# A wait split in two: high products wait for high copies, low products for low copies

## The reference: one decoder layer

```
x = x + attention(layernorm(x))        # 16 heads of 64, causal
x = x + cross_attention(layernorm(x))  # 64 context rows, one head of 256, masked
x = x + ffn(layernorm(x))              # silu gate 256->1024, two gelu layers 1024->1024, 1024->256
```

## Time and profile before

| what | us |
|---|---|
| median of the runs | 1432.95 |
| the profiled execution, its own time | 1431.65 |
| its span (first to last instruction) | 1429.6 |
| TensorE matmul busy | 1414.0 (99%) |
| VectorE busy | 1205.9 (84%) |
| ScalarE busy | 1010.3 (71%) |
| GpSimd busy | 605.3 (42%) |

### The profile page before, as it was taken

How to read it: one execution, slowest core, us unless ns; L and a number is a source line. 1 busy time by engine, 2 the same in 40 slices (tenths; PEclk the granted TensorE clock), 3 DMA queues, 4 the chain that set the end, 5 groups by cost and what they waited for, 6 DMA issues and landing times.

```text
span 1429.6 us, 29169 instructions
## 1 busy us (share of the span) xinstructions
PE 1414.0 (99%) x10408; PEld 1202.3 (84%) x10408; DVE 1205.9 (84%) x3004; ACT 1010.3 (71%) x2382; POOL 605.3 (42%) x883
## 2 busy tenths in 40 slices
PE   8999999999999999999998999999999999999998
PEld 7888888888888888888887788888888888888887
DVE  8998999989989899898899777788866757888886
ACT  7888888888888888888887854565455545555644
POOL 4676777767667767777645121111212100000000
PEclk9999999999999999999999999999999999999999
DMA  5000101001001010010022544553333583141310
GB/s 163 2 1 2 61 1 47 15 2 60 2 16 45 2 61 2 1 61 2 16 75 79 192 157 153 199 176 133 129 129 120 203 299 119 36 144 63 116 58 33
DMA packets 78277, 113.54 MB, mean 79 GB/s; under 512 B 4768, under 2 KB 54304, under 8 KB 77216
## 3 DMA queue, kind: packets, MB, share of 16 engines
q1 hardware_dynamic: 78112, 111.32, 22.7%
HBM read 71.45 MB, written 42.99 MB: 80 GB/s over the span
## 4 chain that ended last, share of the span: by engine, by line
PE 77%; ACT 13%; DVE 6%; issue 2%; POOL 2%; DVEq 0%; ACTq 0%; POOLq 0%
PE bank L1614 14%; PE bank L1446 8%; PE bank L1448 7%; PE bank L877 6%; PE bank L929 6%; ACT P L1012 5%; PE bank L879 5%; PE bank L878 5%; PE bank L1632 4%; PE bank L941 4%; PE bank L954 3%; PE bank L957 3%; ACT PT L981 3%; PE bank L1567 2%; PE bank L1558 2%
## 5 line engine op out<-in xcount | busy, mean ns | idle before, releaser
L1012 ACT ACTIVATE P<-P,stats 128x384 f32<-128x384 f32 (+3 forms) x512 | 290.2, 575 | 101.6 <-DVE stats L1114 100.3
L1144 POOL TENSOR_SCALAR P<-P,stats 128x128 f32<-128x128 f32 (+3 forms) x512 | 268.9, 542 | 113.8 <-DVE stats L1122 111.3
L1114 DVE CUSTOM_DVE_ANT_0 P<-bank,cmask 128x256 f32<-128x256 f32 (+3 forms) x512 | 216.5, 485 | 0.4
L1028 DVE TENSOR_TENSOR PT<-bank,PT 128x512 fp32r<-128x512 f32 (+1 forms) x384 | 206.8, 593 | 7.1 <-ACT PT L981 5.6
L1614 PE MATMUL bank<-op,ws 128*128 128x512 f32 x896 | 205.9, 389 | 0.0
L1446 PE MATMUL bank<-Hb,hw 128*128 128x512 f32 x512 | 201.2, 393 | 0.0
L1614 PEld LDWEIGHTS bank<-op,ws 128*128 128x128 f32 x896 | 167.3, 188 | 34.1
L981 ACT ACTIVATE PT<-bank 128x512 fp32r<-128x512 f32 (+1 forms) x384 | 172.4, 527 | 4.6 <-PE bank L941 3.9
L1448 PE MATMUL bank<-Hb,hw 128*128 128x512 f32 x448 | 174.7, 390 | 0.0
L929 PE MATMUL bank<-K,Q 64*128 64x512 f32 (+3 forms) x1536 | 140.7, 327 | 0.6 <-DVE Q L1028 0.4
L929 PEld LDWEIGHTS bank<-K,Q 64*128 64x128 f32 x1536 | 118.1, 185 | 18.9 <-issue 1.2
(11 more groups left out here) (249 smaller groups left out, 3349.0 us busy)
## 6 DMA issues: line engine op xcount, KB each, us to landing
h_scratch<-go SPq DMA_DIRECT2D x64, 256.0 KB, 2.1
src<-h_scratch SPq DMA_DIRECT2D x16, 1024.0 KB, 7.3
xs<-x_scratch SPq DMA_DIRECT2D x15, 512.0 KB, 4.1
ws<-ws_scratch SPq DMA_DIRECT2D x7, 1024.0 KB, 7.8
x_scratch<-x SPq DMA_DIRECT2D x8, 512.0 KB, 3.0
x_scratch<-xs SPq DMA_DIRECT2D x8, 512.0 KB, 3.3
xg<-x_scratch SPq DMA_DIRECT2D x8, 512.0 KB, 4.6
out<-xg SPq DMA_DIRECT2D x16, 256.0 KB, 2.1
```

The lines of the kernel that those rows point to most:

```text
L1012: e.activation(p, p, ACT.Exp, bias=st_[:, k:k + 1], scale=-1.0, accum_out=st_[:, 8 + k:9 + k]).then_inc(s_exp, 1)
L1028: return e.tensor_tensor(dst, a, b.bitcast(f32), ALU.subtract)
L1114: e.tensor_tensor_reduce(P_tile(P, i, a), banks["S", P, S_ITEM[i]][a][:, slice(*S_COLS[i])], cmask[:, 512 - n:512], -1.0, 3.0e38, ALU.add, ...
L1144: e.tensor_scalar(p, p, stats[P % 4][:, k:k + 1], 1.0, ALU.mult, ALU.mult).then_inc(s_norm, 1)
```

## The change

Only `weighted` is changed. The high product j waits for the high copies of the blocks that it reads, and the low product j for the low copies; the waits ahead of the whole sum are gone. No instruction that computes is added, removed or moved.

```diff
             w.wait_ge(s_vlo, 4 * (P // 4) + 4)
-            for u in (a, 2):
+            for j in range(4):
                 for h in range(2):
-                    w.wait_ge(s_ptlo, plo_at[P, u, h])
-            for j in range(4):
+                    w.wait_ge(s_pthi, hi_at[P, 2 if j == 2 else a, h])
                 e.matmul(out[:, 128 * j:512], V[:, j, P % 4, a * 128:a * 128 + 128],
                          PT[:, a, 0, OFF[j]:OFF[j] + 512 - 128 * j], start=j == 0, stop=j == 3)
             for j in (3, 0, 1, 2):
+                for h in range(2):
+                    w.wait_ge(s_ptlo, plo_at[P, 2 if j == 2 else a, h])
                 m = e.matmul(out[0:64, 128 * j:512], V[:, j, P % 4, a * 128:a * 128 + 64],
                              PT[:, a, 1, OFF[j]:OFF[j] + 512 - 128 * j], start=False, stop=j == 2,
                              skip_group_check=True)
```

## The result

The change makes the kernel slower: 1434.97 us in the median of 22 runs (1433.47 to 1438.8), against 1432.48 (1431.93 to 1433.88) for 22 runs of the kernel before (the three given above are among them). The ratio is 1.0018, with a 95% interval of 1.0012 to 1.0024, so about 2.5 us. The forecast was 1432.5 with a range up to 1434.2, and 0.89 for a difference within 0.2%. The difference is within 0.2%, but the median lies outside the range and on the other side than forecast. The prediction was wrong by a small amount, in the direction of too little cost. It also took 0.2% for what can be told from no change; with 22 runs of each the interval is 0.06% to either side, and leaves no doubt of the sign.

What follows compares the result with a forecast made beforehand. TensorE's matmul stream, busy 99% of the span, was taken as the bound. The median 1432.95 less 0.45 us of kept gain, plus 0 for the added waits, gave 1432.5 us, range 1431.0 to 1434.2.

Steps and rivals of the forecast that it cites:

- Step 1: Weighted sums: the wait for low copies moves to the fifth product in 60 of 64 second sums, mostly stays in first.
- Step 2: Stalls in the weighted sums of pairs 23, 36, 45, 46, 39 and 1: 0.67 us can be won.
- Step 3: Pair 36's first sum: late start and slow group, 0.59 us, stay, as its bank waits for a low copy.
- Step 4: Weighted sums: 128 products gain waits, 85 stand-alone waits are added; price taken as 0, bounds named 1.3 and 11.5 us.
- Step 5: Behind the sums, VectorE can lose earlier starts; two thirds of the 0.67 us counted as kept, 0.45 us.
- Rival A: VectorE, copying without a break at pairs 23 and 36, takes all the gain back: 1432.95 us; chance 0.26.
- Rival B: Added waits at third and fifth products cost weight loads: 11.5 us, 1444.0 us; chance 0.07 past 1436.3 us.
- Rival C: All idle time before line 954, 2.6 us including pair 36's 0.59, is won: 1430.35 us; chance 0.02.
- Rival D: A shifted stream loses or catches a stretch of lowered clock; chance 0.05, divided by sign 0.02 and 0.03.
- The signs of being wrong: In attention: quiet pairs change their step of 11.6 us, or pair 36's stall disappears.

Runs made afterwards that it cites:

- the kernel with the split alone: Changed kernel with its split waits, each product waiting with one condition instead of two, so 6 extra stand-alone waits instead of 85: 1432.04 us, ratio 0.9998.
- 85 late waits: Kernel before plus 85 satisfied stand-alone waits, only in the weighted sums of pairs 53 to 61: 1434.27 us, ratio 1.0015.
- 171 late waits: Changed kernel plus 171 satisfied stand-alone waits in the weighted sums of pairs 53 to 62: 1432.54 us, ratio 1.0000.
- the change with its fetches put back: Changed kernel, all its waits kept, with 42 fewer warm-up transposes (84 instructions) at the program's start: 1432.12 us, ratio 0.9996.
- the waits alone: Kernel before plus 85 satisfied stand-alone waits, in the weighted sums where the change has its own, without the split: 1434.11 us, ratio 1.0014.

## Why the prediction was wrong

**Step 1, where the waits go**, was right: pair 36's first sum still starts late, for the bank's claim.

**Step 2, the 0.67 us that can be won**, was right at each of its places, as the rows of after show.

**Step 3, pair 36's 0.59 us stay**, was right.

**Step 4, the price of the added waits, is the step that failed.** It said "I take 0, as pair 24 is the commoner case and the new waits ask for things that are old". For the time an instruction takes in the queue this was true: the 128 products with new conditions and the 85 stand-alone waits cost nothing inside the sums, and even 256 do not (ratio 1.0002). That a product's second condition on a semaphore makes an instruction of its own is what the two splits show, 446 stand-alone waits against 367. And what the step says of late weights behind a wait is in the trace of before at pair 36: the second product's weight load starts 0.08 us behind the first product (450.65 and 450.57), and in pair 24 0.00 (311.59 and 311.59); the starts of the two products are 0.31 and 0.23 us apart. What the step left out is that instructions have to be brought in (q8: 107 packets, 1.75 MB), and that a transfer of data which a packet meets can land later (the store of `go`, 6.6 us instead of 5.2). The sum had no term for it. It is 1.2 to 1.3 us in the profiles at one place, and 2.5 us in the medians for the change (1434.97 - 1432.48). The row that would have raised the question, q8, was on the page. A reader could not have foretold that the packet hits this store, since the point of each fetch would have had to be followed through the program; but a term with a size (one wait of a microsecond or more, somewhere behind the change) and a chance could have been had. That ought to have gone into the upper bound.

**Step 5, two thirds of the gain kept**, was too hopeful at the three places that were followed. Rival A, with a chance of 0.26, described what happens there: in the kernel with the split alone 0.15 of pair 23's 0.18 us is given back at the next transposes, and all of what pairs 45 and 46 won. The changed kernel gives back the same. For the whole of attention it isn't decided: the kernel with the split alone is at 0.9998, and 0.67 us is too small for the medians to tell how much of it is kept.

**Rival B** was named for the slower side, and it gave the right sign for a wrong reason: quiet pairs have not changed their steps (pair 24: 0.58 and 0.59), and nothing idles before the low products. Nor do the added conditions hold a weight load back there: in pair 24 that of the third product, which now carries one, starts with the product ahead of it (312.56 and 312.55). The size of the additional time is also not its 11.5 us. **Rival C** fell with pair 36. **Rival D**, the clock, did not take place either. The kernel before has a granted clock of 0.50 from 769.1 to 775.9 us (0.51 over 769 to 776), and 0.05 went to a shifted stream that loses this stretch or catches another. The changed kernel has 0.50 from 759.4 to 762.8 and from 773.1 to 776.5, about the same 6.8 us in all, and its mean granted clock is 0.997, as before.

**The signs of being wrong** that the prediction named, a changed step of the quiet pairs and the end of pair 36's stall, did not appear. Both were looked for in attention, where the change is; a loss behind it had no sign of its own.

Of the fetch itself the traces show packets of 16,384 bytes, and the kernel with 256 waits that so many instructions are one packet. TensorE hardly stands still for its instructions: between 100 and 750 us its matmul queue idles once in the kernel before for more than 0.15 us, for 0.35 us at pair 36. A transfer of data that meets the packet is not hidden in the same way. How the packet delays it is the author's estimate, from the packet's 0.9 us and the rate behind it: 23 GB/s is about a sixteenth of the rate ahead, which fits one DMA engine of the sixteen that is late with its share when the others are done. That this engine is the one which brought the instructions is argued, not shown, as the trace doesn't give the engine; nor is it shown why the delay is 1.3 to 1.5 us and the packet only 0.9.

**What stays open.** The profiles of the changed kernel and of the one with 85 late waits show steps of 1.2 and 1.3 us at the place, while their medians lie 2.5 and 2.1 us above the kernel before. The profile is a single execution. Part of the rest comes with the clock that the timed runs were granted. In the runs timed with the late waits the kernel before takes 1431.94 us in the median of its 14 runs at a mean clock of 0.997 or more and 1434.38 in the 7 at 0.996; the kernel with 85 late waits takes 1433.73 (6 runs) and 1436.14 (5 runs). The loss is 1.8 us in either group, and not 2.1. At 0.997 and more the kernel with 171 late waits takes 1432.54 (11 runs), 1.2 us less than the one with 85, which is the size of the step. But the changed kernel, sorted so when it was measured again, lies 2.2 us above the kernel before (1433.79 and 1431.63), so a part of its loss has no place yet. Nor was it tried to take the place itself away, with a third buffer beside the two halves of `go`; a shift might then still hit another transfer.

None of the versions beats the kernel before beyond its interval. The two that had a reason to, the split with one condition and the change with its fetches put back, are at 0.9998 and 0.9996.

## What to carry to other kernels

When a change adds or removes instructions of an engine whose stream is fetched while it runs, it moves the later fetches (here 85 waits in attention moved one from 819.5 to 815.6 us); a difference of 0.1 to 0.2% far from the edit can be this and nothing else, as it was here (1.0014 with the waits alone, 0.9996 with the fetches put back). Before such a difference is given to the edit, find the first place where the streams part, look for a fetch packet beside a transfer that is waited for, and put the fetches back by as many neutral instructions elsewhere (or fill up to a whole packet, 256 instructions here). And a gain of a few tenths of a microsecond ahead of an engine that feeds the next step without slack can be given back there (0.15 of 0.18 us behind pair 23): follow it to the next wait before counting it.

## What the runs showed of the hardware

- The 256 KB store of `go` for which ScalarE waits took 5.2 to 5.3 us from issue to landing in seven kernels, and 6.5 to 6.7 in the five in which a fetch packet of TensorE (16 KB, 0.9 us) started 3.0 to 3.3 us behind its issue. The store issued next took 2.9 to 3.0 us without the packet and 4.3 to 4.5 with it.
- Behind such a packet, in the changed kernel, the DMA engines' rate fell from about 400 GB/s to 23 and stayed there for 1.4 us until the store had landed; in the kernel before, without it, the rate went to nothing in about 0.5 us, for the same 1.57 MB.
- Stand-alone waits that were already satisfied took 0.106 us from one to the next. In one block of 85 they left TensorE idle for 7.78 us where it had idled for 1.67; inside the weighted sums 256 of them cost nothing measurable (ratio 1.0002).
- Two conditions on one semaphore made stand-alone instructions that one condition with the larger count did not: 446 against 367 from the same helper, 85 and 6 more than the 361 before. No weight load carried more than one condition, and no stand-alone wait more than two, in any of the twelve traces.
